# DLRM tower on one core: the loops unrolled, three gather buffers for two, an eighth small table looked up by matmul, and the layers of one pair set between the gram quarters of the next

## The reference

```python
e = jnp.stack([tbl_0[ids[:, 0]], ..., tbl_25[ids[:, 25]]], axis=1)
combined = jnp.concatenate([dense[:, None, :], e], axis=1)          # 2048 x 27 x 128
dots = jnp.einsum('bfd,bgd->bfg', combined, combined)[:, I, J]      # I < J: 351 of them
h = jnp.concatenate([dense, dots, dense], axis=1)                   # 2048 x 607
h = jnp.maximum(h @ W_top1 + b_top1, 0.0)                           # 512
h = jnp.maximum(h @ W_top2 + b_top2, 0.0)                           # 256
y = h @ W_top3                                                      # 1
```

## Time and profile before

| | |
|---|---|
| median of 3 runs | 699.31 us (698.91 to 704.68) |
| profiled execution, span | 696.8 us |
| median less the span | 2.5 us |
| busy: PE, weight loads | 377.1 us (54%), 317.6 us (46%) |
| busy: DVE, ACT, POOL | 209.2 us (30%), 92.9 us (13%), 312.2 us (45%) |
| mean granted clock of PE | 0.740 of full speed |

### The profile page before, as it was taken

How to read it: one execution, slowest core, us unless ns; L and a number is a source line. 1 busy time by engine, 2 the same in 40 slices (tenths; PEclk the granted TensorE clock), 3 DMA queues, 4 the chain that set the end, 5 groups by cost and what they waited for, 6 DMA issues and landing times.

```text
span 696.8 us, 13458 instructions
## 1 busy us (share of the span) xinstructions
PE 377.1 (54%) x5828; PEld 317.6 (46%) x5828; DVE 209.2 (30%) x561; ACT 92.9 (13%) x159; POOL 312.2 (45%) x308
## 2 busy tenths in 40 slices
PE   1306523396284843927349082771817547194897
PEld 1306422394174732717238071561716545083875
DVE  3524007140083100921029010461006600075121
ACT  1111000021011200202002020100201011011132
POOL 6770546304537054470736617174271733637100
PEclk9757755598588775977769595695858858588798
DMA  5651111111101111030101201012010200101000
GB/s 163 189 159 61 41 38 47 31 54 37 41 15 53 64 42 34 21 104 4 49 26 29 100 12 53 16 38 87 20 53 8 98 26 27 49 7 52 19 3 2
DMA packets 18087, 34.32 MB, mean 49 GB/s; under 512 B 8241, under 2 KB 10929, under 8 KB 18065
## 3 DMA queue, kind: packets, MB, share of 16 engines
q0 software_dynamic: 9728, 19.94, 10.0%
q1 hardware_dynamic: 8338, 14.06, 6.1%
HBM read 33.97 MB, written 0.01 MB: 49 GB/s over the span
## 4 chain that ended last, share of the span: by engine, by line
PE 47%; issue 29%; another core or an unknown queue 16%; DMA 4%; ACT 3%; DVE 1%; SPq 0%; ACTq 0%
PE flip_ps L306 15%; PE gram_ps L323 12%; PE flip_ps L290 6%; PE mlp_ps L348 6%; PE mlp_ps L357 5%; DMA raw_then_y<-tbl 4%; ACT feats L456 2%; PE mlp_ps L350 2%; PE mlp_ps L376 1%; ACT hi L619 1%; PE pairs_ps L336 0%; ACT xT L546 0%; ACT xT L549 0%; DVE dots L468 0%
## 5 line engine op out<-in xcount | busy, mean ns | idle before, releaser
L269 POOL DMA_INDIRECT emb<-tbl,idx x304 | 312.0, 1026 | 336.4 <-DMA idx<-ids 225.5
L306 PE MATMUL flip_ps<-marks,hi 125*128 125x256 f32 x448 | 129.6, 321 | 106.0 <-ACT feats L456 102.0
L323 PE MATMUL gram_ps<-feats 128*27 128x27 f32 x4096 | 86.2, 202 | 169.2 <-issue 165.6
L448 DVE COPY feats<-flip_ps 128x512 f32<-128x512 f32 x56 | 38.5, 688 | 400.8 <-remote 247.9
L323 PEld LDWEIGHTS gram_ps<-feats 128*27 128x27 f32 x4096 | 63.7, 113 | 200.1 <-issue 198.6
L306 PEld LDWEIGHTS flip_ps<-marks,hi 125*128 125x128 f32 x448 | 98.8, 220 | 110.9 <-issue 69.7
L484 DVE TENSOR_SCALAR marks<-id_cols,row_no 125x256 fp32r<-125x256 int32 x448 | 127.5, 362 | 32.8 <-remote 25.1
L306 PE MATMUL flip_ps<-marks,lo 125*128 125x256 f32 x448 | 124.6, 310 | 0.9 <-issue 0.9
L306 PEld LDWEIGHTS flip_ps<-marks,lo 125*128 125x128 f32 x448 | 98.7, 220 | 2.1 <-issue 1.8
L290 PE MATMUL flip_ps<-ident,emb 128*128 128x128 f32 x320 | 62.2, 320 | 31.2 <-issue 18.2
L456 ACT COPY feats<-flip_ps 128x512 f32<-128x512 f32 (+1 forms) x32 | 31.5, 984 | 237.0 <-remote 126.1
(11 more groups left out here) (23 smaller groups left out, 77.9 us busy)
## 6 DMA issues: line engine op xcount, KB each, us to landing
id_cols<-ids_in_pairs SPq DMA_DIRECT2D x8, 896.0 KB
emb<-tbl,idx POOLq DMA_INDIRECT x304
emb<-dense SPq DMA_DIRECT2D x16, 64.0 KB
raw_then_y<-tbl SPq DMA_DIRECT2D x2, 500.0 KB
dots<-tbl SPq DMA_DIRECT2D x2, 500.0 KB
h1T<-tbl SPq DMA_DIRECT2D x2, 500.0 KB
w1p_sb<-w_pairs SPq DMA_DIRECT2D x1, 702.0 KB
w_sb<-w SPq DMA_DIRECT2D x1, 512.0 KB
```

The costliest lines, as they stand in the source:

```text
L269: nc.gpsimd.indirect_dma_start(emb[:, u, f, :], None, tables[order[f - 1]][:, :], bass.IndirectOffsetOnAxis(ap=idx[:, u, order[f - 1]:orde ...
L306: last = nc.tensor.matmul(flip_ps[:, m % 2, 2 * (s % 2):2 * (s % 2) + 2, :], part[s][0:R[s], c, :], marks[0:R[s], s % MARK_SLOTS, c, :], s ...
L323: last = nc.tensor.matmul(gram_ps[QUAD * j:QUAD * j + F, n, 0:F], row, row, start=True, stop=True)
L448: copy(feats[:, u, :, GROUP * k:GROUP * k + n], flip_ps[:, m % 2, 0:n, :].rearrange("d f p -> d p f")).then_inc(s_kept[m % 2], 1)
```

## The change

- All loops are written out, on every engine.
- `emb` has three slots, used in turn by tile number; the gather of tile t waits for the transposes of tile t - 3. All ids are loaded at the start.
- Eight tables are looked up by matmul: one of 1,250 rows (ten chunks) joins. 18 are gathered. `marks` has four slots of half a table (up to five chunks each). At the start the raw tables are staged in the third `emb` slot and four other places, so tile 2's gather waits until all tables are split (`s_lo`).
- The dense features are brought to the kernel transposed, loaded once into `dense_sb`, copied to `feats` by ACT (`keep_dense`), and read by layer one directly.
- `flip_ps` has three banks. DVE copies all groups of even tiles, ACT all of odd tiles.
- PE's order: the look-up of group k comes before the transposes of group k, with no layer chunks between; each quarter of the even tile's gram has a chunk of layer one of pair i - 1 ahead of it; the odd tile's gram is in quarters too, with the chunks of layer two, `pair_rows` and layer three between them.
- The result is stored by tiles of 128 samples, all through the run.

```diff
-LOOKED_UP = 7
-GATHERED = F - LOOKED_UP
+LOOKED_UP = 8
+GATHERED = TABLES - LOOKED_UP
+SLOTS = 3
+FLIP_BANKS = 3
...
-        emb = sb("emb", [P, 2, GATHERED, P])
+        idx = sb("idx", [P, tiles, TABLES], i32)
+        dense_sb = sb("dense_sb", [P, batch])
+        emb = sb("emb", [P, SLOTS, GATHERED * P])
...
-        marks = sb("marks", [P, MARK_SLOTS, MAX_CHUNKS, 2 * P], fp32r)
+        id_cols = sb("id_cols", [P, 2, LOOKED_UP, 2 * P], i32)
+        marks = sb("marks", [P, MARK_SLOTS, HALF_CHUNKS, 2 * P], fp32r)
...
+            for t in range(tiles):
+                v = t % SLOTS
+                if t < 2:
+                    pool.wait_ge(s_idx[t], 16)
+                if t == SLOTS - 1:
+                    pool.wait_ge(s_lo, LOOKED_UP)
+                if t >= SLOTS:
+                    pool.wait_ge(s_flip, GROUPS * (t - SLOTS + 1))
+                for k in range(GROUPS):
+                    for f in features_in(k):
+                        nc.gpsimd.indirect_dma_start(
+                            emb[:, v, (f - 1) * P:f * P], None, tables[order[f - 1]][:, :],
+                            bass.IndirectOffsetOnAxis(ap=idx[:, t, order[f - 1]:order[f - 1] + 1], axis=0),
+                        ).then_inc(s_emb[v][k], 16)
...
+            def looking_up(i):
+                for k in range(GROUPS):
+                    if k < LOOK_GROUPS:
+                        look_up(i, k)
+                    if i and k == 0:
+                        pair_rows(2 * i - 1)
+                    flip(2 * i, k)
+            def even_tile(i):
+                if i == 1:
+                    pe.wait_ge(s_weights, 16 * 7)
+                    pe.wait_ge(s_w1d, 1)
+                for part in range(4):
+                    if i:
+                        first_layer(i - 1, BOTH, 2 * (i - 1), range(part, part + 1))
+                    gram(2 * i, part)
+                    if part < GROUPS - 2 or i < pairs - 1:
+                        flip(2 * i + 1, part)
+            def odd_tile(i):
+                flip(2 * i + 1, GROUPS - 1)
+                if i:
+                    second_layer(i - 1, BOTH, range(0, 1))
+                gram(2 * i + 1, 0)
+                if i:
+                    second_layer(i - 1, BOTH, range(1, 2))
+                gram(2 * i + 1, 1)
+                pair_rows(2 * i)
+                gram(2 * i + 1, 2)
+                if i:
+                    third_layer(i - 1, BOTH)
+                gram(2 * i + 1, 3)
+            for i in range(pairs):
+                looking_up(i)
+                even_tile(i)
+                if i < pairs - 1:
+                    odd_tile(i)
+            last = pairs - 1
+            second_layer(last - 1, BOTH)
+            pair_rows(2 * last)
+            third_layer(last - 1, BOTH)
+            first_layer(*LAST[0], 2 * last)
+            flip(2 * last + 1, GROUPS - 2)
+            second_layer(*LAST[0])
+            third_layer(*LAST[0])
+            flip(2 * last + 1, GROUPS - 1)
+            for part in range(4):
+                gram(2 * last + 1, part)
+            pair_rows(tiles - 1)
...
+            for i in range(pairs):
+                if i:
+                    lay_out(2 * i - 1)
+                mark_table(i, 2)
+                keep(2 * i, 0)
+                mark_table(i, 3)
+                mark_table(i, 4)
+                keep(2 * i, 1)
+                mark_table(i, 5)
+                mark_table(i, 6)
+                keep(2 * i, 2)
+                mark_table(i, 7)
+                keep(2 * i, 3)
+                keep(2 * i, 4)
+                if i == 0:
+                    dve.wait_ge(s_weights, 16 * 7)
+                    nc.vector.tensor_tensor(w1d_sb[:, :], w1d_sb[:, :], w1b_sb, ALU.add).then_inc(s_w1d, 1)
+                if i + 1 < pairs:
+                    mark(i + 1, 0)
+                lay_out(2 * i)
+                if i + 1 < pairs:
+                    mark(i + 1, 1)
+                    mark_table(i + 1, 1)
+            lay_out(tiles - 1)
```

More of the change, by code:

```diff
@@ L77, in tower @@
     MAX_CHUNKS = max(N_CHUNKS)
-    dense_v = dense.rearrange("(p t) d -> p t d", t=tiles)
-    ids_v = ids.rearrange("(p t) f -> p t f", t=tiles)
-    out_v = out.rearrange("(p t) o -> o p t", t=tiles)
+    FIRST_CHUNK = [sum(N_CHUNKS[:s]) for s in range(LOOKED_UP)]
+    HALF_CHUNKS = -(-MAX_CHUNKS // 2)
+    assert LOOK_GROUPS == 4 and H1C == 4 and H2C == 2 and GROUPS == 5
     ctx = ExitStack()
@@ L229, in _ @@
                 if s >= PLACES:
                     sp.wait_ge(s_lo, s - PLACES + 1)
[L232 to L236, removed]
+                load_table(s)
@@ L257, in _ @@
+            store(tiles - 4, pairs - 2)
+            store(tiles - 3, pairs - 2)
+            store(tiles - 2, pairs - 1)
+            store(tiles - 1, pairs)
+            for b in range(2):
+                sp.wait_ge(s_out[b], 16 * tiles // 2)
         @block.gpsimd
         def _(pool):
[L259 to L265, removed]
-                    pool.sem_inc(s_open, 1)
-                    for k in range(GROUPS):
-                        for f in tables_in(k):
-                            nc.gpsimd.indirect_dma_start(
-                                emb[:, u, f, :], None, tables[order[f - 1]][:, :],
-                                bass.IndirectOffsetOnAxis(ap=idx[:, u, order[f - 1]:order[f - 1] + 1], axis=0),
-                            ).then_inc(s_emb[u][k], 16)
@@ L312, in gram @@
-            def gram(i, u, rows, first):
-                if rows[0] == 0:
-                    for bank in range(2):
-                        pe.wait_ge(s_kept[bank], kept_before(i, (FLIP[1][0], PER_PAIR)[u], bank))
-                    if not first or u:
-                        pe.wait_ge(s_blocks, 2 * (2 * i + u))
-                for n in rows:
-                    for j in range(P // QUAD):
+                    for x in range(2):
+                        h = 2 * s + x
+                        pe.wait_ge(s_marked, 2 * LOOKED_UP * i + h + 1)
+                        for c in range(half):
+                            for part in (hi, lo):
+                                last = nc.tensor.matmul(
+                                    flip_ps[:, m % FLIP_BANKS, 2 * (s % 2):2 * (s % 2) + 2, :],
+                                    part[s][0:R[s], half * x + c, :],
+                                    marks[0:R[s], h % MARK_SLOTS, c, :],
+                                    start=(x == 0 and c == 0 and part is hi),
+                                    stop=(x == 1 and c == half - 1 and part is lo))
+                        last.then_inc(s_looked, 1)
```

497 lines of the change are left out of this document (216 added, 281 removed).

## The result

The changed kernel takes **705.71 us** (median of 20 runs, 704.34 to 710.5) against 700.67 for the kernel before on the same chip (20 runs, 692.11 to 706.9): a ratio of 1.011, 95% interval 1.0088 to 1.0133. It is slower, by 1.1%: small, but clear of the noise. Each ratio here is taken between runs in the same undisturbed state, so it can differ slightly from the quotient of two medians. The profiled execution has a span of 703.7 us, 6.9 more than before.

A forecast was written before the change was run, and what follows sets the result against it. The prediction took PE and the gather bursts to take turns, PE starving in each burst. Its terms summed to +11.6 us on the profiled 696.8 us, a span of 708.4 and a time of 711 us, range 682 to 732.

The forecast's parts named there:

- (a): Gathers on POOL: 18 a tile in place of 19 take 16 x 1.25 us of starved time away, -20.0 us.
- (b): Look-ups on PE: the eighth table adds 20 matmuls a pair, 2.4 us on PE's own path, +19.0 us.
- (c): Transposes on PE: 32 fewer, as dense features and one table less are transposed, -3.5 us.
- (d): DVE marks in the look-up stretch: fewer marks ahead, imperfect overlap with PE, 1.0 us a pair (bounds 0 and 3), +7 us.
- (e): Unrolling: six former loop passes now fetch instructions, 1.0 us a pair (bounds 0 and 4.5), +6 us.
- (f): PE's work in starved time: about 4.2 us a pair gets through, a loss of 0.6 each, +4 us (bounds -15, +27).
- the second rival: Not slower: the starved time swallows the additions, with two layer chunks through per burst; about 680 us, spread to 700; 27%.
- (g): Third PSUM bank: PE's wait for ACT between look-up groups goes, -4 us (none to -8).
- (h): Start: tile 2's gather waits for the last split and tile 3's follows without pause, one recovery less, -3.3 us.
- (i): Odd bursts: the first gather, no longer held up beside DVE's marks, may starve PE more, +4 us (0 to 9).
- (j): Tail: the last tile's layout of 2.3 us now stands alone after its gram, +2.4 us with the semaphores.
- the first rival: Much faster: gathers do not starve PE, a third buffer lets POOL run through and set the pace, about 400 us; 7%.

The follow-up runs named there:

- seven tables: The changed kernel with seven tables looked up by matmul and 19 gathered, all else kept: 703.16 us, against 702.97 for the changed kernel on the same chip.
- layers first: The changed kernel with the same layer chunks all ahead of each tile's gram quarters: 689.17 us, ratio 1.0116 to the kernel before on the same chip.

## Why the prediction was right, and where it was not

The forecast was 711 us, slower, with a chance of 50% for "slower"; 705.71 came. On the chip of the prediction the view held: **PE starves in every burst**, from shortly after the first gather to 3.4 us after the last, and the change removes no burst. What follows goes by the letters of the prediction.

**(a), (b)** fit. Bursts last 22.2 us in place of 23.4. Seven tables in place of eight, by the terms (a) to (c) +2.8 us before any marks, measured +0.2.

**(d)** is about right for a pair and missed the start. The look-up stretch of a pair takes 19.5 us (405.04 to 424.53), where I had 18.2 and 1.0. PE waits 29.4 us for marks over the run, but 26.1 of them lie in the first 110 us, which (d) left out; in the later look-up stretches it waits twice for some 0.2 us. By seven tables the marks were worth less than the 7 us forecast: 2.6 us, if (a) to (c) hold. The chain of the changed kernel in such a stretch (start, length, what) shows how DVE's copies and marks follow one another with PE behind them:

```profile
239.95 0.73 DVE feats L424
240.69 4.18 DVE marks L460 x16
...
245.51 4.17 DVE marks L460 x16
249.68 0.64 DVE feats L424
250.32 1.03 DVE marks L460 x4
```

**(e)** is the step that was mis-sized. I took 1.0 us a pair, between none and two stops of 2.3. The stops exist in the kernel before, which is 12.7 us slower when it is unrolled. In the changed kernel there are none between the bursts: from 170 to 670 us no gap of PE's issue in a free stretch exceeds 0.35 us, though q8 moved 29 packets from 215 to 630 us, where it had moved none. Why is open. The layer chunks between the quarters are one guess, but layers first has none between those of the even tile, only transposes, and shows no such stop between its bursts from 170 to 600 us either; and the run without gathers, with the chunks in place, has gaps of up to 0.92 us. Only the last gram, with neither layers nor transposes in it, shows the long stops, and two for one before:

```profile
682.44 1.22 PE L304 MATMUL gram_ps<-feats 128*27 128x27 f32 x122 [0.48 <-ACT feats L424]
...
685.22 1.27 PE L304 MATMUL gram_ps<-feats 128*27 128x27 f32 x128 [1.56 <-issue]
...
688.95 0.31 PE L304 MATMUL gram_ps<-feats 128*27 128x27 f32 x6 [2.46 <-issue]
```

1.56 + 2.46 less 2.27 makes +1.75 us in place of +6. That is 4.3 us less than forecast, in a measured span that is 4.7 below the forecast one of 708.4. It is not the whole account, as the sum by place below shows.

**(f)** had the right mechanism: a burst lets a number of instructions through. It counted too little on both sides. In the changed kernel two layer chunks get through each burst and not one (the second stands at 436.06 to 444.04 in the even burst), which was the condition of the second rival; and in the kernel before the odd burst also let a layer chunk and transposes through, and lost its time to the wait for ACT shown above. Layers first shows that large matmuls ahead of gram are worth 13.8 us, which is not the order of the change.

**(g)** PE no longer waits for ACT between look-up groups. **(h)** Tiles 2 and 3 are gathered in one burst, 63.9 to 108.8. **(i)** All first gathers of later bursts take 0.94, so the gather that used to lie still beside DVE's marks now goes like the others, the case of the upper bound of 9 and not of the 4 I took; its price was not measured by itself. **(j)** `pair_rows` of the last tile waits 2.47 us for DVE; I had 2.4. The tail as a whole is nonetheless 5.4 us shorter, since it holds one burst fewer.

**A pair** was to last 86 us. Over five pairs it is 85.0, against 84.1 before. By the terms of the forecast a pair was to grow by 2.1 us, so five pairs by 10.4, and start and end by the other 1.2; measured are 4.8 and 2.1. Of the 1.2 us a pair that did not come, (e) is 1.0. (d) went 0.3 the other way, which leaves (f), (g) and (i) together 0.5 lower than forecast (an estimate by subtraction); they can't be told apart.

So the side was right for the reason given, that no burst goes; its size is in part luck. The sum adds a gain of 20 and a cost of 19 with eight small terms, of which several were off with either sign.

What was incomplete lies deeper than a term. I wrote that PE and the gathers take turns, and treated that as a property of the program. It holds on two further chips and not on a third. There the first rival, "the buffers work", is the right picture (its 400 us stand beside the 405 estimated above), and by that estimate the change would make the kernel faster by some 4 to 5%. Nothing in the trace of before could tell that, because it holds one chip. **Open** stays why PE starves on some chips and not on others. These two traces of one program show the same gathers, the same issue times on POOL (0.94 + 0.30) and the same bytes. They differ in PE's mean granted clock too, 0.740 against 0.891, but that looks like a consequence: in layers first it is 1.00 until the starving sets in and 0.59 behind it. What else sets the chips apart, or whether it is the chip or its condition at that time, these traces don't tell. It was not tried to run the changed kernel on the third chip, nor the kernel before on every one.

## What to carry to other kernels

Read a large "issue" share on a chain against the timeline of the gathers; where the two line up, count the instructions that get through a burst, and put the largest matmuls and not the most numerous ones there (2.0% here). Before you shape a kernel around such a wait, run it on more than one chip: the same program took 424 and 700 us, and a third buffer that was worth 2 us on one seems the main part of a gain of 8 on another. A loop whose body needs no fetch is worth leaving a loop until a run says otherwise; unrolling cost this kernel 1.9%.

## What the runs showed that I had not expected

- One program differs by a factor of 1.6 between chips. 159 of the 275 us of span between the two traces are gram's issue waits (165.6 against 6.2 us), and 80 the look-ups' waits for ACT's copies (102.0 against 21.7). Its runs on one chip spread over some 2% or less (692 to 707, 676 to 691, 422 to 426 us).
- On a starving chip a burst of 18 gathers lets 89 to 98 matmuls through in some 25.4 us, in the pairs shown of the changed kernel and of layers first, whether some 15 or some 31 of them are large ones of the layers.
- A burst holds up ACT's copies too: one whose input was done at 464.7 us began at 483.06, 3.3 us after the last gather.
- Indirect gathers starve PE; plain loads of the same size from the same engine (0.54 us each) do not, and neither do the same bytes landing from loads that SP issues.
- An indirect gather costs POOL 1.21 us with 64 rows and 1.25 with 128.
- An unrolled gram with nothing between its matmuls stops for 1.3 to 2.6 us; with layer chunks or transposes between its quarters no gap over 0.35 us was seen between bursts, up to 0.92 us where there were no bursts. That the fetch makes the stops is argued, not shown.
